# Maxima of the natural scores over four PSUM banks in one VectorE instruction

## The reference

```python
bias = jnp.concatenate([alibi, alibi], axis=-1)
ssm_mask = (delta >= 0) & (delta < W_SSM)      # W_SSM = W_ATT = 64, T = 256
scores = jnp.einsum('bhqd,bhkd->bhqk', q, k) / np.sqrt(D).astype(np.float32)
scores = jnp.where(mask[None, None], scores + bias[None], -jnp.inf)
wei = jax.nn.softmax(scores, axis=-1)
```

## Time and profile before

| what | value |
|---|---|
| median of three runs | 942.38 us |
| profiled execution | 940.1 us |
| its span, first to last instruction | 938.3 us |
| PE busy | 807.2 us, 86% |
| DVE busy | 517.6 us, 55%, 1061 instructions |
| ACT busy | 323.9 us, 35% |
| POOL busy | 86.0 us, 9% |
| mean granted TensorE clock | 0.976 |

### The profile page before, as it was taken

The page is one execution under the profiler, slowest core; times in us unless marked ns, Lnnn a source line. Parts: engine busy times, 40 slices in busy tenths (PEclk is TensorE's granted clock), DMA queues, the critical chain, the costliest instruction groups (busy, mean ns, idle before and its releaser), DMA issues.

```text
span 938.3 us, 22588 instructions
## 1 busy us (share of the span) xinstructions
PE 807.2 (86%) x10182; PEld 523.8 (56%) x10227; DVE 517.6 (55%) x1061; ACT 323.9 (35%) x422; POOL 86.0 (9%) x103
## 2 busy tenths in 40 slices
PE   3787787889899889989899889989898988998996
PEld 3453664358645775458645774457634864474443
DVE  4636467445955578446945477437846374425233
ACT  5352122533243332442244323452244324330322
POOL 1102002000120002000210012000110001010001
PEclk9998999999999899999999899999999899999999
DMA  9552000000001000010001000010001000000000
GB/s 347 189 86 51 1 2 24 2 24 2 1 24 45 2 2 24 1 46 2 2 24 46 2 2 24 1 47 2 1 1 46 2 2 1 23 2 1 1 23 22
DMA packets 18878, 27.06 MB, mean 29 GB/s; under 512 B 5464, under 2 KB 7640, under 8 KB 18784
## 3 DMA queue, kind: packets, MB, share of 16 engines
q1 hardware_dynamic: 18640, 25.61, 9.0%
q10 hardware_dynamic: 144, 0.03, 0.0%
HBM read 21.44 MB, written 4.19 MB: 27 GB/s over the span
## 4 chain that ended last, share of the span: by engine, by line
PE 61%; DVE 19%; ACT 14%; issue 4%; POOL 1%; DMA 1%; ACTq 0%; POOLq 0%; SPq 0%; DVEq 0%
ACT p_b L740 8%; DVE max_b L1446 7%; PE ps L1107 7%; PE ps L1143 6%; PE ps L1028 5%; PE ps L1184 5%; PE ps L1011 4%; PE ps L1072 3%; PE ps L1048 3%; PE ps L935 3%; PE ps L862 2%; PE ps L1116 2%; PE ps L945 2%; PE ps L1036 2%; PE ps L948 2%
## 5 line engine op out<-in xcount | busy, mean ns | idle before, releaser
L740 ACT ACTIVATE p_b<-ps 128x2048 f32<-128x2048 f32 x64 | 106.5, 1664 | 116.9 <-PE ps L1116 116.9
L1446 DVE TENSOR_REDUCE max_b<-ps 128x4 f32<-128x768 f32 (+2 forms) x160 | 106.5, 710 | 43.4 <-PE ps L1084 23.7
L1107 PE MATMUL ps<-q_b,k_b 32*128 32x512 f32 (+1 forms) x512 | 66.2, 586 | 14.1 <-ACT p_b L740 8.0
L1072 PE MATMUL ps<-k_b,q_b 32*128 32x192 f32 (+2 forms) x1024 | 55.7, 332 | 24.3 <-DVE max_b L1446 22.1
L1472 DVE STREAM_TRANSPOSE o_nat<-ps 128x512 f32<-128x512 f32 x32 | 21.0, 695 | 84.9 <-PE ps L1132 84.9
L1011 PE MATMUL ps<-c_t,wq 128*128 128x256 f32 x256 | 60.7, 385 | 3.6 <-DVE out_a L1369 2.7
L1132 PE MATMUL ps<-p_b,v_b 128*32 128x256 f32 (+1 forms) x1024 | 61.7, 358 | 2.1 <-ACT p_b L740 2.0
L1326 DVE SCALAR_TENSOR_TENSOR nat<-ps,st_a,qkv_bias 128x512 f32<-128x512 f32 x48 | 35.3, 739 | 50.7 <-PE ps L862 50.5
L1072 PEld LDWEIGHTS ps<-k_b,q_b 32*128 32x128 f32 x1024 | 39.2, 184 | 41.8 <-DVE max_b L1446 35.5
L1184 PE MATMUL ps<-base_t,x_t 128*128 128x512 f32 x128 | 61.7, 608 | 0.1
L1028 PE MATMUL ps<-x_t,wq 128*128 128x256 f32 x256 | 59.9, 384 | 0.0
(11 more groups left out here) (191 smaller groups left out, 1430.1 us busy)
## 6 DMA issues: line engine op xcount, KB each, us to landing
x_in<-x SPq DMA_DIRECT2D x8, 512.0 KB, 3.6
p_b<-ctx SPq DMA_DIRECT2D x8, 512.0 KB, 4.3
y<-x SPq DMA_DIRECT2D x7, 512.0 KB, 3.0
p_b<-L_attn_qkv_w SPq DMA_DIRECT2D x2, 1024.0 KB, 6.5
p_b<-L_xattn_Wq SPq DMA_DIRECT2D x1, 2048.0 KB, 14.7
x<-L_attn_qkv_w SPq DMA_DIRECT2D x2, 512.0 KB, 9.5
x<-L_ffn_base_w SPq DMA_DIRECT2D x2, 512.0 KB, 7.2
wo<-L_xattn_Wo SPq DMA_DIRECT2D x8, 128.0 KB, 7.0
```

The costliest lines, as they stand in the source:

```text
L740: act.activation(p_b[:, j % 2, :, 0:cols], ps[:, 4:8, 0:cols], ACT.Exp, scale=DB ** -0.5).then_inc(pb_here.sem, 1)
L1072: pe.matmul(bank(4 + r)[:, (i % 2) * N:(i % 2) * N + 2 * n * S], q_b[strip[r], i, :, :].rearrange("p h q -> p (h q)"), k_b[strip[r], half, ...
L1107: pe.matmul(bank(4 + r)[:, 0:nb * P], k_b[strip[r], half, 2 * j:2 * j + 2, :, :].rearrange("p c s k -> p (c s k)"), q_b[strip[r], 2 * j:2 ...
L1446: ins = dve.tensor_reduce(max_b[:, half, 0, i:i + k, 2 * n:2 * n + 2], ps[:, 4 + 2 * n:6 + 2 * n, :].rearrange("p r (i n) -> p i r n", i=2 ...
```

## The change

The call with n = 0 returns at once. The call with n = 1 waits for all four banks and reduces them together: 1536 elements on each partition, and at pair 0 two instructions of 256 and 512. `sb_max` then rises by 2, so the counts for which TensorE and `b2_max` wait stay as they are. The lists are not changed.

```diff
             def b2(b, half, pair, n):
-                    sb_full(dve, b, 8 * half + 2 * pair + n + 1)
+                    if n == 0:
+                        return
+                    sb_full(dve, b, 8 * half + 2 * pair + 2)
                     for i in ((2 * pair, 2 * pair + 1) if pair == 0 else (2 * pair,)):
                         k = 1 if pair == 0 else 2
                         cols = 2 * S * (min(i, 2) + 1)
-                        ins = dve.tensor_reduce(max_b[:, half, 0, i:i + k, 2 * n:2 * n + 2],
-                                                ps[:, 4 + 2 * n:6 + 2 * n, :].rearrange("p r (i n) -> p i r n", i=2)[:, i % 2:i % 2 + k, :, 0:cols],
+                        ins = dve.tensor_reduce(max_b[:, half, 0, i:i + k, :],
+                                                ps[:, 4:8, :].rearrange("p r (i n) -> p i r n", i=2)[:, i % 2:i % 2 + k, :, 0:cols],
                                                 AX.X, ALU.max)
-                    ins.then_inc(sb_max.sem, 1)
+                    ins.then_inc(sb_max.sem, 2)
```

## The result

| | us | runs |
|---|---|---|
| before | 942.38 median (940.92 to 942.97) | 5 |
| changed | 946.56 median (944.96 to 948.62) | 5 |
| ratio | 1.0047, 95% interval 1.0029 to 1.0066 | |

The changed kernel is slower by 4.2 us; I forecast 1.2 and called "no change" the likeliest. 946.56 us lies just inside the stated range (940.2 to 946.6) and outside the forecast's own (942.0 to 945.2). One execution further down, the profiled one of e7_ms_behind, took 1632.32 us and is left out of that kernel's median.

A forecast was written before the change was run, and what follows sets the result against it. The prediction took a chain of waits between TensorE (busy 86%) and VectorE as the bound. Five steady batches at +0.46 gave +2.3 us, batches 0, 6 and 7 -1.1: net +1.2, 943.6 us, range 940.2 to 946.6.

The forecast's parts named there:

- no change: Whole kernel: the time stays within about 0.2% (1.9 us), what a measurement tells from no change; chance 0.57.
- The hole: At (half 0, pair 2), batches 1 to 5: VectorE idles ahead of line 1385, making line 1392 later by 0.80 us.
- B: The hole at line 1385 doesn't decide, since something else would hold line 1019 or maxima (1, 0); 939.6 us, chance 0.11.
- The savings of the merge: Merged maxima on the chain: 0.07 us saved behind VectorE's own work, 0.04 behind TensorE, more at pair 0.
- 0.03 us of banks: Maxima behind TensorE: the merged one must wait for all four banks, the pair's last two matmuls, 0.03 us.
- pair 0: Maxima of pair 0: four instructions become two, saving 0.13 us, or 0.10 where VectorE waits for TensorE.
- Rival D: Merged maxima: each merge saves the whole fixed 0.15 us of an instruction; all -3.4 us, 939.0 us, chance 0.04.
- A: Merged maxima: reading four banks in one instruction saves nothing; a steady batch +0.93, all +5.0 us, 947.4 us, chance 0.10.
- C: TensorE late in a batch: later work makes two of three short low-clock stretches long, 1.0 us each; 945.6 us, chance 0.15.

The follow-up runs named there:

- e7_ms_behind: The changed kernel with line 1385 behind the merged maxima (0, 2) in batches 1 to 5; 947.31 us, ratio 1.0057.
- e1: The kernel before, nothing merged, with line 1385 ahead of both halves of (0, 2) in batches 1 to 5; 949.11 us, ratio 1.0069.
- e2: The changed kernel, but (0, 2) of batches 1 to 5 stays in two halves around line 1385; 941.22 us, ratio 0.9988.
- e4: The kernel before with one idle reduction between maxima (0, 3) and line 1458 in batches 1 to 5; 946.30 us, ratio 1.0040.
- e9: Line 1385 ahead of both halves of (0, 2), in the kernel before with idle matmuls in TensorE's waits; 936.06 us, ratio 0.9930.
- e10: An idle reduction behind maxima (0, 3), in the kernel before with idle matmuls in TensorE's waits; 934.22 us, ratio 0.9916.
- the filled pair: The kernel before and the changed kernel, each with idle matmuls in two TensorE waits of five batches; 931.84 us and 936.11 us.

## Why the prediction was wrong

**The hole, right.** +0.80 at (0, 2) was forecast; line 1392 came 0.79 later. e1 makes it without a merge, e2 takes it away and with it the loss. B, that it would be hidden, is refuted. The Trainium skill's advice in Perfetto Trace Analysis, Optimizing Scalar/DVE Operations, that breaking instructions up may help where Vector makes bubbles on other engines, holds in this trace at just this place, with 0.79 us.

**The savings of the merge, the term that failed.** I took -0.07 behind VectorE's own work and -0.04 behind TensorE, as if a longer reduction started as soon after its wait as a short one, but for 0.03 us of banks. The durations are right, but a long reduction that follows a wait starts 0.12 later behind TensorE (0.05 banks, 0.07 its form), so there the merge loses 0.04 (3.12 to 3.16) in place of gaining 0.04. At (0, 3), which waits for line 1399, it starts 0.09 after that line's end in place of 0.03 and gains nothing. Only pair 0 gains as forecast, and instructions in a queue without a wait. Most of a steady batch's miss is behind (1, 0) and (1, 1), -0.17 in the sum: in batch 4 TensorE's matmuls for (1, 3) do begin 0.13 earlier (8.07 us behind (1, 0) for 8.20), but the merged (1, 3) starts 0.14 behind them where the first half started 0.03 behind. I had counted the savings at (1, 3) as hidden and its late start at nothing.

The sums: a steady batch +0.65 in place of +0.46; batches 0, 6 and 7 from (0, 0) to (1, 3) +0.05, -0.22 and +0.16, together nothing, in place of -1.1. In all, 5 x 0.65 = +3.2 in place of +1.2. Rival D, and with it the estimate by the Trainium skill's 125 ns (same page, same section), went the wrong way. A, at +5.0, came nearest in size for another reason: it had the durations unchanged and a steady batch at +0.93.

**The clock, a rival that should have been in the sum.** I had C at 0.15 because stretches may as well shorten. One did, but three grew: three of six were long before, five after, five with e4, six with e1. I priced one at 1.0 us from a single pair of batches; over the five steady periods of the trace before, one with a long stretch takes 0.9 to 1.4 us more than one with a short one. The 4.5 us between the two profiled spans are 3.2 and some 1.3 for a net two. Batch by batch that is uneven: of the two periods with a long stretch in both kernels, one grew by 0.2 us and one by 1.0, which stays open. In the medians of e1 and e4, 2.9 and 1.7 us stand above the local sums, and nothing does once TensorE's waits are filled (e9, e10). For the changed kernel itself the mean granted clock fell like e4's (0.973 over its five executions, 0.976 before), but the filled pair gave 3.2 by its traces and 4.3 by its times. So the clock's share in its 4.2 us, some 1 us, is likely and not shown by the times.

## What to carry to other kernels

Before two instructions are merged, look at what stands between them in their engine's queue: a half that runs in another instruction's wait costs nothing, and merged it costs the length of the wait that it had filled, here 0.79 us. Count the start after a wait, not only the duration, since here it took all that the merge saved but at pair 0. And where TensorE's clock falls after each idle stretch, a later arrival can cost more than its length (7.0 us for 4.1 in e1); filling the waits gained 10 us where the change had cost 4.2.

## What the hardware showed

One VectorE reduction over four PSUM banks took 1.046 ns for each element that it has more than the form over two (950 ns for 768, 1753 for 1536), the same as within the forms over two (1.045). Behind a wait for all four banks, one reduction of 1536 elements started 0.07 us later than the first of two of 768 (1.41 for 1.34), whichever way it read the banks. Idle matmuls in 2.7 and 1.3 us of TensorE's waits kept the granted clock at 2.4 GHz where it had fallen to 1.2, and took 2.3 us out of a batch whose low stretch was long (104.7 to 102.38) and 1.3 where it was short (103.7).
